# P times V in bursts of two key tiles at every second pair, and the copy-out three exponentials later

## The reference

```
x = x + 0.5 * ffn(layernorm(x))
x = x + attention(layernorm(x))
x = x + 0.5 * ffn(layernorm(x))
```

```
scores = einsum('bhqd,bhkd->bhqk', q, k) / sqrt(8)
out    = einsum('bhqk,bhkd->bhqd', softmax(scores), v)
```

## Time and profile before

| what | value |
|---|---|
| median of 3 runs | 816.57 us (816.46 to 821.61) |
| the profiled execution | 818.14 us |
| its span | 816.3 us |
| mean granted TensorE clock | 0.939 of full speed |
| PE matmul busy | 743.4 us (91%) |
| VectorE busy | 751.1 us (92%) |
| ScalarE busy | 622.2 us (76%) |
| GpSimd busy | 239.5 us (29%) |

### The profile page before, as it was taken

How to read it: one execution, slowest core, us unless ns; L and a number is a source line. 1 busy time by engine, 2 the same in 40 slices (tenths; PEclk the granted TensorE clock), 3 DMA queues, 4 the chain that set the end, 5 groups by cost and what they waited for, 6 DMA issues and landing times.

```text
span 816.3 us, 17968 instructions
## 1 busy us (share of the span) xinstructions
PE 743.4 (91%) x6952; PEld 263.8 (32%) x6953; DVE 751.1 (92%) x977; ACT 622.2 (76%) x1144; POOL 239.5 (29%) x498
## 2 busy tenths in 40 slices
PE   4876668999999999899999999999999899998992
PEld 2663542222222222222222222222222222233572
DVE  6889989999999999999999999999999999975583
ACT  1222762599999999799999997999999799995620
POOL 2634520132222322232232223223222232324121
PEclk9997875699999999899999999999999899998987
DMA  4000000000000000000000000000000000000000
GB/s 110 1 1 1 0 1 0 1 5 6 4 6 5 8 6 6 5 5 5 6 5 5 6 6 5 5 5 8 6 4 6 5 5 6 5 6 4 4 27 26
DMA packets 17905, 6.73 MB, mean 8 GB/s; under 512 B 11424, under 2 KB 17184, under 8 KB 17824
## 3 DMA queue, kind: packets, MB, share of 16 engines
q1 hardware_dynamic: 7280, 3.77, 1.7%
q0 software_dynamic: 8192, 1.19, 1.0%
q10 hardware_dynamic: 2352, 0.66, 0.4%
HBM read 2.23 MB, written 1.05 MB: 4 GB/s over the span
## 4 chain that ended last, share of the span: by engine, by line
DVE 64%; PE 21%; issue 8%; POOL 3%; ACT 1%; DMA 1%; DVEq 1%; POOLq 0%; SPq 0%; ACTq 0%
DVE mh L707 56%; PE ps L1075 8%; PE ps L1062 5%; PE ps L1047 3%; PE ps L917 1%; PE ps L979 1%; DVE terms L731 1%; PE ps L1022 1%; DMA X<-in_L_attn_x_dram 1%; DVE ring L658 1%; POOL XB L340 1%; DVE X L668 1%; DVE terms L663 1%; DVE top L715 1%; ACT QT L869 1%
## 5 line engine op out<-in xcount | busy, mean ns | idle before, releaser
L883 ACT ACTIVATE ring<-ps 128x512 f32<-128x512 f32 x1024 | 551.3, 599 | 63.9 <-PE ps L1062 46.0
L707 DVE TENSOR_REDUCE mh<-ps 128x2 f32<-128x1024 f32 x512 | 585.1, 1213 | 8.2 <-PE ps L1047 8.0
L1075 PE MATMUL ps<-ring,Vx 128*32 128x256 f32 x4096 | 332.3, 397 | 0.2
L1047 PE MATMUL ps<-KT,QT 48*128 48x512 bf16 x1024 | 211.6, 397 | 11.9 <-DVE mh L707 11.9
L1062 PE MATMUL ps<-QT,KT 51*128 51x512 bf16 x1024 | 216.3, 392 | 0.9
L430 POOL DMA_DIRECT2D terms<-outT x128 | 65.5, 519 | 248.0 <-ACT outT L891 230.3
L1075 PEld LDWEIGHTS ps<-ring,Vx 128*32 128x32 f32 x4096 | 81.2, 108 | 162.2 <-ACT ring L883 141.0
L1062 PEld LDWEIGHTS ps<-QT,KT 51*128 51x128 bf16 x1024 | 53.3, 93 | 225.2 <-ACT ring L883 205.5
L419 POOL DMA_DIRECT2D QT<-mrow x128 | 72.3, 570 | 40.8 <-DVE mrow L724 40.1
L1047 PEld LDWEIGHTS ps<-KT,QT 48*128 48x128 bf16 x1024 | 50.2, 94 | 61.3 <-DVE mh L707 25.5
L407 POOL TENSOR_TENSOR mp<-zeros,top 128x8 bf16<-128x8 f32 x32 | 6.3, 197 | 171.6 <-DVE top L715 171.6
(11 more groups left out here) (108 smaller groups left out, 368.3 us busy)
## 6 DMA issues: line engine op xcount, KB each, us to landing
QT<-mrow SPq DMA_DIRECT2D x128, 0.8 KB
QT<-mrow POOLq DMA_DIRECT2D x128, 0.8 KB, 1.7
terms<-outT SPq DMA_DIRECT2D x128, 8.0 KB
terms<-outT POOLq DMA_DIRECT2D x128, 8.0 KB, 1.6
out_dram<-X SPq DMA_DIRECT2D x4, 256.0 KB, 2.3
wfc_n<-in_L_ffn_W_fc_dram SPq DMA_DIRECT2D x1, 256.0 KB, 3.4
wpj_n<-in_L_ffn_W_proj_dram SPq DMA_DIRECT2D x1, 256.0 KB, 3.8
rope<-rope_tables ACTq DMA_DIRECT2D x1, 128.0 KB, 5.6
```

The costliest lines, as they stand in the source:

```text
L707: v.tensor_reduce(mh[:, n // A_STEP % 2, :, q, kb], ps[:, bank:bank + 2, :], AX.X, ALU.max)\
L883: a.activation(ring[:, n % PRING, :], ps[:, EXP[n % C_EXP], :], ACT.Exp, scale=SCALE).then_inc(p_ready, 1)
L1047: mm = t.matmul(ps[:, A0 + 2 * (n % 2) + h, :], QT[rows, j, at:at + P], KT[rows, j, kb * CS:(kb + 1) * CS], start=True, stop=True)
L1075: mm = t.matmul(ps[r:r + 32, PO, 0:QH], Vx[:, kt, col:col + 32], ring[:, (2 * n + h) % PRING, half * QH:(half + 1) * QH], start=(kt == 0), ...
```

## The change

`pv_tile` is no longer issued once behind every pair. It is issued twice in a row behind every second pair, for the tiles three and two pairs back. The number of matmuls and their shapes stay as they are. `take_out` moves from behind the third exponential of the next group (k = 2) to behind the sixth (k = 5).

```diff
-OUT_AT = 2
+OUT_AT = 5
...
                     if k % 2 and n + 2 * LEAD < 2 * UNITS:
                         max_mm(n - 1 + 2 * LEAD)
                         max_mm(n + 2 * LEAD)
-                    if k % 2 and n // 2 >= PV_LAG:
+                    if k % 4 == 3 and n // 2 > PV_LAG:
+                        pv_tile(n // 2 - PV_LAG - 1)
                         pv_tile(n // 2 - PV_LAG)
                     if (g, k) in LATE:
                         late(*LATE[g, k])
```

## The result

The changed kernel takes 907.46 us (median of 4 runs, 903.08 to 908.81), the kernel before 816.52 beside it. The ratio is 1.109, with a 95% interval of 1.105 to 1.113. The forecast was 903 us, 878 to 928.

A forecast was written before the change was run, and what follows sets the result against it. VectorE bounds the kernel before; after, PE with its wait for ACT. The terms 631 + 7 + 12 - 570.5 + 7 give +86 us, so span 902.5, execution 904.4, median 903 us, range 878 to 928.

The forecast's parts named there:

- The bound before: Attention stage before the change: VectorE sets the pace at 1.15 us a pair, with PE full at 1.10 us.
- The wait for ACT: After the change, second head's scores wait for the previous pair's first exponential until 1.07 us; PE idles 0.41 us.
- A: In the changed attention stage, the pair without P times V behind it; its scores are time 0.
- B: In the changed attention stage, the pair after A, with two tiles of P times V behind it.
- double pair: A and B together, the repeating unit of the changed attention stage: forecast 2.61 us, bounds 2.52 to 2.70.
- What is removed: PE, per two pairs: one change-over into P times V (0.09), one out (0.11), one first pass (0.02); 0.22 us together.
- first rival: Attention stage: the wait for ACT doesn't show, PE needs 2.20 us, VectorE stays bound at 2.30; 816 us; 6%.
- The copy-out: In each of 30 groups, the next group's first P times V tile waits 0.2 us for ACT's copy; 7 us.
- From pair 4 to pair 487: Main attention stretch: 570.5 us before; after, 631 us, plus 7 for copy-outs and 12 for three reciprocals.
- the last 25 pairs: End of attention, without maxima: 4.6 us from slower pairs, 1.7 from a later transpose, 0.6 from the last tiles; 7 together.
- The change-over is not moved into the bursts: Denies a rival: each run of two P times V tiles pays the change-over inside; 2.8 us per two pairs, 950 us; 3%.
- The clock did not fall in the steady part: Denies a rival: PE's 0.4 us pauses drop its clock to half; about 4.0 us per two pairs, some 1240 us; 4%.

## Why the prediction was right

**The bound before.** VectorE first, PE 0.05 us a pair behind it. Shown: with VectorE's reductions halved the old order falls to 1.11 us a pair and no further, and the bursts don't move at all. PE's 1.11 us is its own, since the chain there holds no wait for ACT; the loop would allow 1.07.

**The wait for ACT.** Forecast 1.07 us from A's scores to the second head's of B, and a double pair of 2.61. Measured 1.08 and 2.61 to 2.62 (a group, with the copy's 0.2, takes 21.12 us, which is 8 x 2.61 + 0.2). The three lengths of the exponential show that this loop is the bound, and the maxima brought together show that it is the missing cover that exposes it.

**What is removed.** Forecast 0.22 us on change-overs, given back by the 0.22 of scores that no longer stream side by side: 2.20 us of PE's own work in either order. The old order measured 2.22. For the bursts the sum of the distances fits (0.45 and 0.22 up to the second head's scores if they didn't wait, 0.53 to P times V, 1.00 out of it), but no run shows it alone; the nearest took 2.29 with 0.10 of wait left in it. The prediction's first rival has 2.20 us of work with no wait at all. By its own terms that should be 1.98, since it is the wait that parts the two heads' scores; VectorE's 2.30 would have been the bound in both cases.

The Trainium skill, "TensorEngine Tiling (Array Packing)", Key Properties, says that a change of tiling mode drains the array. The distances agree with it (into P times V 0.52 - 0.22 = 0.30 us behind the last of the maxima's matmuls, and 0.33 out of it, where neighbours of one kind are 0.22 apart). No burst kernel shows a double pair under the old order's 2.22 us, so halving the number of changes brought nothing in time here.

**The copy-out.** Forecast 0.2 us a group in the bursts: moving it one exponential earlier took 0.21 off a group. Alone, 0.63 expected, 0.70 measured.

**The stretches.** From pair 4 to pair 487 the forecast was 631 + 7 + 12 = 650 us. The timeline has these pairs here:

```profile
154.83 0.39 PE L1062 MATMUL ps<-QT,KT 51*128 51x512 bf16 x2
...
804.13 0.38 PE L1062 MATMUL ps<-QT,KT 51*128 51x512 bf16 x1
```

804.13 - 154.83 = 649.3 us, so +78.8 against the earlier trace rows (the prediction's 241.5 x 2.61 is 630.3 and not 631, which changes nothing). The copy-outs and the reciprocals are in it. The three groups with a reciprocal took 24.2, 26.5 and 25.3 us, 12.6 over three ordinary ones (12 forecast). 483 pairs at 21.12 for 16 are 637.6; with the 12.6 that is 0.9 more than the 649.3, since pair 487 is a pair B and starts 0.45 us behind its A, not half a double pair.

**The term that was mis-sized** is the last 25 pairs: +7 us forecast, +11.9 measured. From pair 487 to the end of P times V the kernel before took 36.7 us, the changed one 48.7. The transpose came 828.93 - 818.92 = 10.01 us behind the last group's first scores, just as forecast (10.0). What I left out is the clock behind it. I had read the 3.82 us pause of the kernel before and its 10 us at full clock later, and let the stretch in between be the same in both. It wasn't: at half clock for 20 us, a double pair takes 3.70 us in place of 2.40. Taking the pause away gave 11.3 us back. With the start 0.9 us earlier and the rest behind the attention 0.9 us shorter, the sum is 78.8 + 11.9 - 0.9 - 0.9 = 89 us, against 86.

**The range** is narrower than the bounds it names. The double pair's 22 us, the reciprocals' 5 down and 3 up and the copy-out's 7 down and 8 up, all at their ends at once, give 869 to 936. 878 to 928 takes less than that, and the prediction doesn't say how; 907 lies well inside either.

**The rivals.** The wait does show. The change-over is not moved into the bursts: 16 rows of P times V take 1.07 us; the starts of its four passes are 0.24, 0.22 (the seam of the two tiles) and 0.22 apart. The clock did not fall in the steady part. It was full from 154.7 to 363.0 us and, apart from the stretches behind the reciprocals, up to 827.2. A stretch of 100 us with all its pauses:

```profile
400.00:500.00 100.00, 89.67 (x912) 27.86 (x904) 90.33 (x84) 79.52 (x158) 23.39 (x57) 1.00 0.03 5
```

The Trainium skill, "TensorE: Matmul & The Clock Gate", A second HAM failure mode: psum-queue depth-cycling, would have had it swing; pauses of 0.4 us in every 2.6 didn't do that here. The signs that I named were less exact than the time: VectorE's idle time rose to 65 us (80 forecast), ACT's to 186 (150 forecast).

## What to carry to other kernels

Before instructions are gathered into bursts, ask what each of them hides where it stands: a latency loop (scores, exponential, bank free again) that is a little shorter than the pace costs nothing until its cover is moved away, and then it costs in full. Lay the loop out from single rows, hand-overs included, and compare it with the work that is left between its ends; here that gave the new pace to 0.01 us. And price a pause of some us by the clock behind it as well, in the order that follows it, and with a spread: equal pauses were followed by half clock of unequal length.

## What the runs showed of the hardware that was not expected

An exponential over 128, 256 and 512 columns took 0.28, 0.38 and 0.60 us. Worked out from these, it is about 0.17 us fixed and 0.83 ns a column.

How long the half clock lasts after a pause differs much, with pauses that are nearly alike. In the kernel before it held for 7 us behind 3.82 us of waiting; in the changed kernel for 20 us behind 4.71; with the maxima together and with 256-column exponentials, both behind 4.70, for 30 and for 27. The rows of the last two, in this order:

```profile
784.00:814.00 30.00, 26.42 (x150) 8.40 (x151) 7.90 (x15) 13.22 (x26) 6.12 (x8) 0.50 0.00 1
```
```profile
768.00:795.00 27.00, 25.11 (x148) 7.86 (x148) 7.48 (x15) 7.91 (x24) 5.52 (x7) 0.50 0.00 1
```

The changed kernel and these two run the last pairs in bursts, and all burst kernels with that pause had 10 us of half clock or more behind it. But single traces can't say how much of the length belongs to the order. In the changed kernel's own trace, the three reciprocals each hold PE for the same 1.79 us, and the half clock behind them lasts 3.4, 10.2 and 6.8 us. The first two:

```profile
363.00:366.40 3.40, 3.17 (x24) 0.80 (x22) 3.11 (x3) 1.09 (x2) 0.00 (x0) 0.50 0.00 0
537.10:547.20 10.10, 10.10 (x63) 2.41 (x56) 6.36 (x6) 5.22 (x11) 2.05 (x4) 0.50 0.03 7
```

Why one pause is left sooner than another was not settled; the runs show only that without the pause in the last group the same bursts keep the full clock.
